# A five-layer attention stack: batch-owned buffers, a written-out order, seven shared PSUM banks, maxima in groups of heads

## The reference

```python
# phase 0: cross attention with rotary positions, keys from ctx
q = rope(x @ Wq.T + bq); k = rope(ctx @ Wk.T); v = ctx @ Wv.T + bv
x = softmax(q k^T * scale) v @ Wo.T + bo + x
# phase 1: layer norm, modulation by a vector from ctx, attention within each half of 128 tokens
x0 = x0 + g_msa * mha(mod(ln(x0)));  x1 = x1 + g_msa * mha(mod(ln(x1)))
# phase 2: queries of one half, keys of the other half; then an MLP 128 -> 512 -> 128 with gelu
x = x + g_mca * (attend(q0, k1, v1), attend(q1, k0, v0)) @ Wo + ...
x = x + g_mlp * mlp(mod(ln(x)))
# phase 3: cross attention with ctx, and the layer norm after it
x = ln(softmax(q k^T / sqrt(8)) v @ Wo.T + bo + x) * gamma + beta
# phase 4: layer norm, cross attention with ctx, weights rounded to -1, 0, 1 times their mean size
x = x + softmax(q k^T * scale) v @ bit(Wo).T + bo
```

## Time and profile before

| | |
|---|---|
| median of 3 runs | 361.76 us (361.42 to 364.45) |
| profiled execution, span from first to last instruction | 356.7 us |
| instructions | 8841 |
| TensorE busy | 303.9 us, 85% |
| weight loads busy | 169.3 us |
| VectorE busy | 246.3 us, 69% |
| ScalarE busy | 233.3 us, 65% |
| GpSimd busy | 187.3 us, 53% |
| SP's queue | DMA issues, 120 + 120 of stacks, 44 of maxima |

### The profile page before, as it was taken

The page is one execution under the profiler, slowest core; times in us unless marked ns, Lnnn a source line. Parts: engine busy times, 40 slices in busy tenths (PEclk is TensorE's granted clock), DMA queues, the critical chain, the costliest instruction groups (busy, mean ns, idle before and its releaser), DMA issues.

```text
span 356.7 us, 8841 instructions
## 1 busy us (share of the span) xinstructions
PE 303.9 (85%) x3162; PEld 169.3 (47%) x3162; DVE 246.3 (69%) x551; ACT 233.3 (65%) x491; POOL 187.3 (53%) x273
## 2 busy tenths in 40 slices
PE   3187899789899689788988989899888999898993
PEld 2173444345436466556666656455343534344331
DVE  2679599989746657758738487857686879778411
ACT  1131275767878378576768586787787777676782
POOL 3876498968888555336254332403676675740000
PEclk9587699999999899899899989879999999999999
DMA  2769700303032122133132111200212112130000
GB/s 70 184 164 244 249 9 5 83 10 79 16 83 68 33 75 75 50 77 91 27 91 54 39 47 48 60 9 19 74 38 58 51 41 69 37 78 18 17 17 16
DMA packets 40563, 22.95 MB, mean 64 GB/s; under 512 B 4872, under 2 KB 39688, under 8 KB 40392
## 3 DMA queue, kind: packets, MB, share of 16 engines
q1 hardware_dynamic: 39832, 22.30, 23.9%
q0 software_dynamic: 256, 0.07, 0.2%
q10 hardware_dynamic: 432, 0.02, 0.1%
HBM read 5.79 MB, written 0.52 MB: 18 GB/s over the span
## 4 chain that ended last, share of the span: by engine, by line
PE 30%; DVE 6%; ACT 6%; POOL 5%; issue 5%; SPq 1%; DMA 1%; POOLq 0%; ACTq 0%; DVEq 0%
PE ps_small L937 9%; PE ps_heads L937 7%; PE ps_max L937 5%; PE ps_score L937 5%; POOL normed L735 3%; ACT probs L1155 2%; DVE neg_max L1294 2%; PE ps_small L1108 2%; POOL rstd L908 1%; PE ps_small L1112 1%; DVE stats L1258 1%; PE ps_small L1122 1%; SPq L793 1%; DVE normed L735 1%; ACT L1228 1%
## 5 line engine op out<-in xcount | busy, mean ns | idle before, releaser
L1294 DVE TENSOR_REDUCE neg_max<-ps_max 128x2 f32<-128x512 f32 (+1 forms) x256 | 159.8, 682 | 38.4 <-PE ps_max L937 37.7
L1155 ACT ACTIVATE probs<-ps_score 128x512 f32<-128x512 f32 x256 | 141.4, 600 | 29.5 <-PE ps_score L937 28.5
L937 PE MATMUL ps_score<-q_stack,k_stack 64*128 64x256 bf16 (+1 forms) x640 | 78.8, 258 | 6.6 <-ACT probs L1155 4.3
L937 PE MATMUL ps_heads<-probs,v_cols 128*32 128x256 f32 (+1 forms) x1280 | 83.1, 350 | 0.6 <-ACT probs L1155 0.4
L937 PE MATMUL ps_max<-k_stack,q_stack 62*128 62x256 bf16 (+1 forms) x640 | 72.0, 259 | 7.9 <-DVE neg_max L1294 4.1
L937 PEld LDWEIGHTS ps_score<-q_stack,k_stack 64*128 64x128 bf16 x640 | 34.1, 96 | 40.9 <-ACT probs L1155 29.0
L937 PEld LDWEIGHTS ps_max<-k_stack,q_stack 62*128 62x128 bf16 x640 | 33.3, 96 | 41.2 <-DVE neg_max L1294 22.8
L937 PEld LDWEIGHTS ps_heads<-probs,v_cols 128*32 128x32 f32 x1280 | 28.3, 109 | 25.4 <-issue 17.3
L702 POOL TENSOR_TENSOR split_r<-q_f,k_parts 128x256 f32<-128x256 f32 x19 | 12.8, 673 | 46.2 <-issue 41.9
L937 PE MATMUL ps_small<-src_t,w 128*128 128x256 f32 x96 | 30.0, 433 | 0.9 <-issue 0.5
L908 POOL TENSOR_TENSOR rstd<-var_eps,minus_half 128x2 f32<-128x2 f32 x20 | 14.2, 708 | 30.8 <-DVE var_eps L1263 30.6
(11 more groups left out here) (112 smaller groups left out, 420.6 us busy)
## 6 DMA issues: line engine op xcount, KB each, us to landing
k_stack<-k_parts SPq DMA_DIRECT2D x120, 64.0 KB, 2.1
q_stack<-q_parts SPq DMA_DIRECT2D x120, 64.0 KB, 2.1
w<-in_w SPq DMA_DIRECT2D x1, 1024.0 KB, 5.8
rows<-in_rows SPq DMA_DIRECT2D x1, 704.0 KB, 5.0
w<-in_w SPq DMA_DIRECT2D x1, 576.0 KB, 8.6
q_stack<-max_rows SPq DMA_DIRECT2D x36, 8.0 KB
ctx_t<-in_ctx_t SPq DMA_DIRECT2D x4, 128.0 KB, 3.5
src_t<-in_x_t SPq DMA_DIRECT2D x4, 128.0 KB, 3.6
```

The source lines that it names most:

```text
L937: return nc.tensor.matmul(out, lhs_t, rhs, start=start, stop=stop, **k)
L1155: nc.scalar.activation(probs[:, n % PROB_BUFS, :], ps_score[n % SCORE_BUFS][:, :], ACT.Exp, scale=SCALE).then_inc(exped, 1)
L1294: nc.vector.tensor_reduce(dst, src, AX.X, ALU.max, negate=True).then_inc(max_taken, 1)
```

## The change

The whole recording of steps is written anew; what is computed stays the same.

- **Order.** `make_schedule`, `Plan` and `WEIGHTS` go. A string `ORDER` of 1,959 two-letter steps sets the order: a letter for a stream, a digit for the batch. A step now belongs to one engine (`take_max` on VectorE is apart from `max` on TensorE), so each engine's place is set separately. Within a batch the streams keep their order; between batches it is free.
- **Buffers.** Everything that belonged to a unit by `u % 2` or `u % 3` is now one buffer for each batch, and tiles are reused within a batch (`heads_normed` holds normalised heads and the normed tile, `rope_gated_o` the gathered rotary rows and later the gated weights).
- **Banks.** `BANK_OF` names for each product one of seven shared banks; the value sums keep the eighth.
- **Groups.** All full-key units hand their maxima over in two groups of eight heads, the last unit in four groups.
- **Coupled products.** Where `COUPLED` says so (170 pairs), two products of the max or score kind are issued in turns, matmul by matmul.
- **Work moved.** The norm's apply and epsilon: GpSimd, in all phases (24 instructions of the apply move there). Splits of maxima: GpSimd in phases 0 (but unit 0) and 3, VectorE in 1, 2 and 4. The first unit's key split goes from VectorE to GpSimd; the sum of the rotation of batches 1 to 3 too. The copy of transposed maxima: VectorE in phase 4, ScalarE in the others. Six stack transfers of the first unit's q are issued by ScalarE.
- **Start.** The four `spare` transfers become eight memsets on VectorE. The rotary table is stored wide, so it is gathered wide (1 KB a row) and not widened. The gates are one 8-row product, stored to memory and read back to all rows; the gates of the MLP are no longer folded into the weights but multiplied behind it.

The core of the diff (the order is 35 lines of such strings):

```diff
-SLOTS = ((0, 2), (1, 1), (2, 0), (0, 1), (1, 0), (0, 0))
+SLOTS = ((0, 2), (0, 1), (0, 0), (1, 0), (2, 0), (1, 1))
...
-SPARE_SLOTS = (6, 7)
...
-STACK_BUFS = 3
 BANK = 512
-CHUNK = BANK
-SMALL_BUFS, MAX_BUFS, SCORE_BUFS = 2, 3, 2
+BANKS = 8
 VALUES = 8
 PROB_BUFS = 8
-GROUPED = (0, UNITS - 1)
-
-SPLIT_ON_DVE = ()
-ON_DVE = (("max_split", 0), ("max_split", 1), ("max_split", 2), ("max_split", 3), ("max_split", 4),
-          ("max_t", 1), ("max_t", 4),
-          ("norm", 0), ("norm", 1), ("norm", 2))
+
+
+
+FIRST, LAST = (0, 0), (PHASES - 1, B - 1)
+GROUPS = {(p, b): 2 for p in (0, 3, 4) for b in range(B)} | {LAST: 4}
+
+
+MAX_T_ON = ("act", "act", "act", "act", "dve")
+APPLY_ON = ("pool", "pool", "pool", "pool")
+SPLIT_MAX_ON = ("pool", "dve", "dve", "pool", "dve")
+
...
+    "Q0K0R0z0r0r0k010R1z1Q1q0y000y00000i0K1i0W0r1d1R2z2r1d1k1i1K2r2d21010Q2r2k2i1d2q11111M0m0M0m021j1M0m0M0M0m0m0M0q2"
...
+BANK_OF = (
+    "0122021342430562430564123056516032104361420363024161423065132346051202364501326532503610524302615340631426203520"
...
+COUPLED = (
+    "0101000000001000010010000001001010001010000010101001001010001010101010101010000001001000000010101010100010101010"
...
+def make_steps():
+    waiting = {letter + str(b): list(steps) for b in range(B) for letter, (_, steps) in streams(b).items()}
+    steps = []
+    for n in range(0, len(ORDER), 2):
+        kind, p, i = waiting[ORDER[n:n + 2]].pop(0)
+        steps.append((kind, p, int(ORDER[n + 1]), i))
+    assert not any(waiting.values())
+    return steps
...
+    row_steps = [st for st in steps if st[0] in ("max", "score")]
+    couple = {}
+    for n, st in enumerate(row_steps):
+        if COUPLED[n] == "1":
+            couple[row_steps[n - 1]] = st
...
-        q_stack = sb("q_stack", [P, STACK_BUFS, PAIRS, T], BF16)
-        neg_max = sb("neg_max", [P, 2, NT, 2, PAIRS])
+        q_stack = sb("q_stack", [P, B, PAIRS, T], BF16)
+        neg_max = sb("neg_max", [P, B, NT, 2, PAIRS])
...
-        ps_max = [ctx.enter_context(nc.psum_tensor(f"ps_max{i}", [P, BANK], F32)) for i in range(MAX_BUFS)]
-        ps_score = [ctx.enter_context(nc.psum_tensor(f"ps_score{i}", [P, BANK], F32)) for i in range(SCORE_BUFS)]
-        ps_heads = ctx.enter_context(nc.psum_tensor("ps_heads", [P, BANK], F32))
-        ps_smalls = [ctx.enter_context(nc.psum_tensor(f"ps_small{i}", [P, BANK], F32)) for i in range(SMALL_BUFS)]
...
+        rope_gated_o = sb("rope_gated_o", [P, 2 * B, 2, D])
+        rope_hidden = sb("rope_hidden", [P, B, 2 * T])
+        gates_dram = nc.dram_tensor("gates_dram", [2 * B * 3 * D], F32).ap()
+
+        ps = [ctx.enter_context(nc.psum_tensor(f"ps{i}", [P, BANK], F32)) for i in range(BANKS)]
...
+        def place_parts(queue, kind, p, b, part):
+            if part == 0:
+                queue.wait_ge(stacks_preset, 2 * (b + 1))
+                if p:
+                    queue.wait_ge(*done("score", p - 1, b, n_banks(p - 1) - 1))
+            queue.wait_ge(*part_ready(kind, p, b, part))
+            stack, sem_ = (q_stack, q_placed[b]) if kind == "q" else (k_stack, k_placed[b])
+            for slot, slot_parts in enumerate(SLOTS):
+                if slot_parts[kind == "k"] == part:
+                    queue.dma_start(stack[slot::ROW_SLOTS, b, :, :], parts_of(kind, b)[part]).then_inc(sem_, 16)
...
+        def split_part(engine, ops, link, rest, kind, p, b, i):
+            part, full = parts_of(kind, b), q_f[:, b, 0 if kind == "q" else 1, :]
+            step = ("split_" + kind, p, b, i)
+            if i == 0:
+                engine.wait_ge(*part_ready(kind, p, b, 0))
+                ops.tensor_tensor(part[1], full, part[0], ALU.subtract).then_inc(of(step), 1)
+            else:
+                link(ops.tensor_tensor(rest, full, part[0], ALU.subtract))
+                engine.wait_ge(*part_ready(kind, p, b, 1))
+                ops.tensor_tensor(part[2], rest, part[1], ALU.subtract).then_inc(of(step), 1)
+                engine.wait_ge(*done(*step))
...
+                    if p < 2:
                         pool.wait_ge(w_loaded[1], 16)
-                    link(nc.gpsimd.tensor_tensor(gates[:, i, :, :], gates[:, i, :, :],
-                                                 rows[:, R_AT["gate1"]:R_AT["gate3"] + 1, :], ALU.add))
-                    nc.gpsimd.tensor_tensor(gate_bias[:, i, :, :], gates[:, i, :, :],
-                                            rows[:, R_AT["bo1"]:R_AT["bfc2"] + 1, :], ALU.mult)
-                    for j in range(2):
-                        nc.gpsimd.tensor_tensor(gated_o[:, i, j, :], W(f"o{j + 1}"), gates[:, i, j, :], ALU.mult)
-                    nc.gpsimd.tensor_tensor(gated_fc2[:, i, :, :], w[:, W_AT["fc2a"]:W_AT["fc2d"] + 1, :],
-                                            gates[:, i, 2:3, :].broadcast_to([P, 4, D]), ALU.mult).then_inc(gate_folded, 1)
...
+                        pool.wait_ge(*done("rope", 0, b, 0))
+                        for qt in range(NT):
+                            last = nc.gpsimd.tensor_tensor(rope_gated_o[:, 2 * b + qt, p, :], W(f"o{p + 1}"),
+                                                           gates[:, 2 * b + qt, p, :], ALU.mult)
+                        link(last)
+                        g = gates[:, 2 * b:2 * b + 2, p, :]
...
+            def inverse_deviation(p, b, i):
+                pool.wait_ge(*done("stats", p, b, i))
+                link(nc.gpsimd.tensor_scalar(var_eps[:, b, :], mean_var[:, b, :, 1], 1e-5 if p == 3 else 1e-6, None, ALU.add))
+                link(nc.gpsimd.tensor_tensor(rstd[:, b, :], var_eps[:, b, :], minus_half[:, :], ALU.pow))
...
+                if kind in ("max", "score"):
+                    row_wait(st)
+                    other = couple.get(st)
+                    if other:
+                        row_wait(other)
+                    n = 4 if halves(p) else 2
+                    for j in range(n):
+                        last = row_multiply(st, j)
+                        if j == n - 1:
+                            last.then_inc(of(st), 1)
+                        if other:
+                            last = row_multiply(other, j)
+                            if j == n - 1:
+                                last.then_inc(of(other), 1)
...
+            def preset_stacks(b):
+                nc.vector.memset(q_stack[:, b, :, :].rearrange("p e t -> p (e t)"), 0.0).then_inc(stacks_preset, 1)
+                nc.vector.memset(k_stack[:, b, :, :].rearrange("p e t -> p (e t)"), 1.0).then_inc(stacks_preset, 1)
```

1735 lines of the change are left out of this document (705 added, 1030 removed).

## The result

The changed kernel takes 324.38 us (median of four runs: 319.23, 319.85, 328.91, 329.58); the kernel before took 361.59 in the same comparison. The time relative to before is **0.891, 95% interval 0.881 to 0.901**. The profiled execution of the changed kernel is the one of 319.23 us; its span is 317.4 us.

A forecast was written before the change was run, and what follows sets the result against it. Order, buffers and latencies were taken to set the pace, TensorE nearest to full. Start 39.1 + middle 277 (301.4 - 21 + 3.6 - 7) + end 8.3 = 324.4 span; plus 5.1 gives 329.5, forecast 329 us, range 308 to 348.

The forecast's parts named there:

- rival A: Whole kernel: the terms add up, ScalarE at 78 to 84% in the middle, 320 to 342 us; chance 0.50.
- Every sign that the prediction named: First exponential at 38 to 41 us, ScalarE 78 to 84%, idle weight loading under 17.3, TensorE's score-bank wait below 29.0.
- The start: Before the first exponential: SP's queue delays the first maxima; issued at 35.8 us, first exponential at 39.1, 8.2 earlier.
- The presets: VectorE's stack memsets before the rotation: no delay taken, 2 us kept for the range; GpSimd's clears hide some 7 us.
- -21 for 100 fewer layout changes: TensorE in the middle: 412 array layout changes become 312, each saving 0.21 us of idle weight loading.
- -7 for the banks: TensorE in the middle: seven shared banks remove a quarter of its 29.0 us wait for score banks; ends 0 and 29.
- Coupling 0: TensorE's 170 coupled pairs in the middle: worth 0 us, with 0.1 each, 17 us, as the upper end.
- The other engines fit: In a 277 us middle, ScalarE fills 81%, VectorE 72%, GpSimd 67%; none becomes the bound by its sum.
- Rival C: Middle: layout changes removed in phases 1 and 2 are hidden; only full-key stages gain, 339 to 346 us; chance 0.21.
- Rival E: Norm on GpSimd delays norms and splits, up to 116 us if all exposed; slower, 381 at 45% exposed; chance 0.09.
- The rule on shared access: VectorE's 20 two-input products on maxima wait for GpSimd's SBUF reads: 4.7 us, as before; at worst 14, time 340.
- The way from span to time: Whole kernel: 5.1 us added to the forecast span, the distance of the earlier median 361.76 from its span 356.7.

The follow-up runs named there:

- e_lateweights: The changed kernel with SP issuing two large weight loads behind the first unit's first maxima, not ahead of the second unit's keys; 324.0 us, 0.905 of the kernel before.
- f_earlymax: The kernel before with the transfer of the first unit's first maxima moved ahead of two weight loads and twelve stack transfers on SP; 356.6 us, 1.002.
- e_shift: The changed kernel with 29 whole runs of value steps (56 steps) moved behind the next product or pair, layout changes still 312; 338.1 us, 0.942.
- e_swap: The changed kernel with 32 value steps moved behind the next product or pair, 376 layout changes instead of 312; 330.7 us, 0.923.
- e_oldall: The changed kernel with the order and engine assignment of the kernel before; new buffers, shared banks and start kept; 356.0 us, 1.002.
- e_bankslru: The changed kernel with only the bank table replaced: each product gets the shared bank free longest in the list; 338.8 us, 0.955.
- e_banks322: The changed kernel with its seven shared banks cut into three for maxima, two for scores, two for the rest, 257 steps moved; 432.4 us, 1.210.
- e_oldorder: The changed kernel with the order of the kernel before, uncoupled, banks by longest free; new engines, buffers and shared banks kept; 374.7 us, 1.048.
- e_normdve: The changed kernel with the norm's apply of phases 0 to 2 (24 instructions) back on VectorE; 347.8 us, 0.978.
- e_split: The changed kernel with 51 runs of value steps broken up (66 steps later), 400 layout changes, banks by longest free; 378.1 us, 1.058.

## Why the prediction came out as it did

The time forecast was 329 (308 to 348) and 324.4 was measured; rival A, "the sum", holds by its numbers, at their lower edge (320 to 342, against the median of 324.4 and the mean of 319.5). The span was forecast at 324.4 and measured at 317.4: 1.4 us more than forecast at the start, 8.1 less in the middle, 0.3 less at the end. Every sign that the prediction named came out, and yet its reasons hold much less well. That the largest term, 21 us, fell near the gain of the middle is luck as far as its reason goes.

- **The start: 39.1 forecast, 40.5 measured; the cause only half right.** GpSimd's end (20.4 for 21.0) and SP's issue (35.74 for 35.8) came as worked out; the first exponential followed 4.8 us later instead of 3.3, because SP's transfer took longer to land beside the two large weight loads (e_lateweights, without them, is back at 3.3). But "SP's queue holds it up" is refuted as the one cause by f_earlymax. The gain came since the change also takes the six gate products and the next unit's maxima out of TensorE's queue ahead of the first score.
- **The presets: right.** No delay was counted, and there is none at the end, though they took longer than the nearest row. Three pairs ran from 5.76 to 15.2 us, 9.4 us, with 0.91 and 1.76 us for each pair plus gaps of 0.16 and 0.38, and the rotation came at 15.16, 2.8 later; GpSimd's clears hid it. The Trainium skill (VectorE: DVE Perf Modes, Zero memsets can be issued as uint32) led to an estimate of 9.6 us for three pairs: the trace agrees with it, at 3.2 us from the start of one pair to the next (5.76 to 8.97), and not with the copy at 0.695.
- **The middle: 277 forecast, 268.9 measured.** The term "-21 for 100 fewer layout changes" is the step that failed as a reason: a moved value step costs as much in e_shift without more changes as in e_swap with two more for each (0.33 and 0.35 us). "-7 for the banks" can't be a number of its own: 0 in the old order with banks by the rule (e_oldall), 19 for the choice among the same seven (e_bankslru), over 100 with three kinds and 257 moved steps (e_banks322). "Coupling 0" came out 6 too low in the time, and right in phase 3, where the clock was the same. "+3.6 for transposes" was not tested alone; the busy time of the maxima's transposes rose by 3.4 (6.2 to 9.6).
- **The other engines fit: right.** ScalarE's work in the middle is 218.7 (225.6), at 81% as forecast; VectorE's 202.3 (200). GpSimd's whole is 203.6 (214): the folding of gates shrank from 33.0 us (10.1 + 8.0 + 8.0 + 6.9) to 15.7 (7.0 + 5.8 + 2.9), 17 and not the 10 that was counted.
- **Rival C: the place of the gain is refuted.** It held that the layout changes of phases 1 and 2 lie in the shadow of the batch's chain, so that only full-key stages gain. Phases 1 and 2 gained 22.5 of the 32.5 us, and full-key phase 3 nothing.
- **Rival E: wrong for this order, real in the old one.** 19 us by e_oldorder against e_oldall, the norm with three other kinds of work; in the changed kernel it is VectorE that would cost 28.
- **The rule on shared access: the chain did not suffer.** The 20 splits' products on VectorE take 0.283 us on average, 5.7 us in all, and in the kernel before 22 of them took 0.329, 7.2 in all. So long ones are there before and after, and the row of 0.18 from which 4.7 us were reckoned is one of the short ones. The step from 14 us to "329 + 11" has no working that gives 11.
- **The end: 8.0 for 8.3. The way from span to time: mis-sized.** 5.1 us were added, the distance of the median of before from its profiled span; the same distance is 7.0 after the change. The profiled execution itself lies 1.8 above its span.

What carried the gain, as a ladder of measured kernels: old order, engines, groups with new buffers and banks 356.0; the work moved, 374.7; the new order with its groups and pairs, 338.8; its bank table, 319.5. The middle steps belong together: taken out of the finished kernel one at a time, table, pairs, engines and places cost 6 to 28 us each, 72 in all with e_shift's, and the whole gain is 37 to 39; of those that were put into the old order, buffers and banks gain nothing, and the moved work and the groups lose. What in the order does it (which places, which groups) stays open.

## What to carry to other kernels

In this kernel, where every engine works through one queue, the gain of a searched order could not be split into prices per part: what was taken out singly adds up to twice the gain. What held was the share of the middle that ScalarE's work fills (81%). Before a late transfer is called the cause of a late start, see what else stands in the waiting engine's queue, and whether it waited at all: here TensorE came to its first score product at 46.85 us with the late transfer and at 47.11 with the early one. And change such an order only together with its bank table and its engines: 32 value steps moved behind one product cost 11 us here, 56 cost 19.

## What was unexpected about the hardware

- The granted clock differs with the order: kernels with the same matmuls (3,172 in each) ran at means of 0.949 (the change), 0.928 (e_bankslru), 0.901 (e_normdve) and 0.885 (e_split), and TensorE's busy time grew from 273.8 to 303.0 us.
- Row products issued in turns gain nothing where the clock is the same: TensorE is busy for 62.48 us of phase 3 with 49 such pairs and for 62.72 without, as the earlier trace rows (0.39 for two matmuls, 0.40 for four) would have it.
- Additions over two columns (0.228 us) and the two instructions of a split over 16 (0.197 and 0.222) on GpSimd are close to the 0.25 that was taken. The splits are below VectorE's own over 16 columns in the changed kernel (0.334 and 0.295).
